# The first four heads scored in pairs, two key tiles of one pair in a step

## What is computed

```python
# x: (8, 512, 256)   ctx: (8, 1601, 256)   16 heads of 16 columns
q = split_heads(layernorm(x) @ Wq.T + bq)
k = split_heads(ctx @ Wk.T + bk)
v = split_heads(ctx @ Wv.T + bv)
attn = softmax(einsum('bhqd,bhkd->bhqk', q, k) / 4)
x = x + merge_heads(einsum('bhqk,bhkd->bhqd', attn, v)) @ Wo.T + bo
gate, y = fp4_linear(layernorm(x), w_gate), fp4_linear(layernorm(x), w_up)
x = x + fp4_linear(silu(gate) * y, w_down)   # 704 wide, blocks of 16 rounded to FP4
```

## Time and profile before

| what | value |
|---|---|
| median of 3 runs | 1728.53 us (1728.46 to 1728.66) |
| the profiled execution | 1727.77 us |
| its span, first to last instruction | 1725.6 us |
| PE busy | 1653.8 us, 96% of the span |
| DVE busy | 1428.7 us, 83% |
| ACT busy | 1132.9 us, 66% |
| mean granted TensorE clock | 0.989 |
| first score product | 69.89 us into the span |

### The profile page before, as it was taken

One profiled execution on the slowest core, in us unless ns is written; L12 is line 12 of the kernel. 1 busy time (PEld: TensorE's weight loads), 2 busy tenths in 40 slices (PEclk: granted clock), 3 DMA queues, 4 the chain that ended last, 5 costly groups with the idle time before them and its releaser, 6 DMA issues.

```text
span 1725.6 us, 27107 instructions
## 1 busy us (share of the span) xinstructions
PE 1653.8 (96%) x9484; PEld 665.2 (39%) x9484; DVE 1428.7 (83%) x2084; ACT 1132.9 (66%) x2295; POOL 548.5 (32%) x661
## 2 busy tenths in 40 slices
PE   6799899999999999999999999999999999989978
PEld 4332234334433344333443344333443344323345
DVE  5878988988798978898889887899878987898347
ACT  3377677766777667776677667776677766666731
POOL 5238520732025320543107320263304431013301
PEclk9899999999999999999999999999999999999989
DMA  6735332431335333142323323243222323200000
GB/s 164 164 76 136 70 70 44 107 93 33 56 66 120 63 63 57 49 116 46 78 45 85 102 41 58 48 118 85 57 55 55 79 48 67 45 8 10 13 22 13
DMA packets 106772, 117.53 MB, mean 68 GB/s; under 512 B 23237, under 2 KB 88141, under 8 KB 106637
## 3 DMA queue, kind: packets, MB, share of 16 engines
q1 hardware_dynamic: 101808, 111.62, 30.6%
q10 hardware_dynamic: 4828, 4.18, 1.0%
HBM read 76.78 MB, written 30.16 MB: 62 GB/s over the span
## 4 chain that ended last, share of the span: by engine, by line
PE 82%; DVE 11%; ACT 4%; issue 2%; DMA 1%; POOL 0%; ACTq 0%; SPq 0%; DVEq 0%
PE pvb L871 21%; PE st L837 20%; PE mx L856 11%; PE misc L758 7%; DVE cmx L1120 5%; PE misc L720 5%; PE misc L713 4%; PE misc L779 3%; ACT prob L1042 2%; PE misc L771 2%; PE misc L699 2%; PE misc L767 1%; PE misc L799 1%; PE misc L808 1%; DVE ht L1149 1%
## 5 line engine op out<-in xcount | busy, mean ns | idle before, releaser
L1042 ACT ACTIVATE prob<-st 128x512 f32<-128x512 f32 (+1 forms) x1591 | 867.4, 599 | 374.8 <-PE st L837 371.4
L1120 DVE TENSOR_REDUCE cmx<-mx 128x2 f32<-128x1024 f32 x768 | 905.1, 1219 | 149.5 <-PE mx L856 144.2
L837 PE MATMUL st<-qstack,kstack 112*128 112x512 bf16 (+1 forms) x1591 | 497.0, 384 | 8.9 <-ACT prob L1042 2.4
L871 PE MATMUL pvb<-prob,vv 128*32 128x512 f32 (+1 forms) x3328 | 444.2, 606 | 0.6 <-ACT prob L1042 0.6
L837 PEld LDWEIGHTS st<-qstack,kstack 112*128 112x128 bf16 (+1 forms) x1591 | 128.1, 98 | 464.8 <-issue 238.3
L856 PE MATMUL mx<-kstack,qstack 48*128 48x512 bf16 (+1 forms) x2048 | 256.5, 336 | 17.5 <-DVE cmx L1120 17.4
L1377 POOL TENSOR_TENSOR ht<-ht,rh 128x352 f32<-128x352 f32 (+1 forms) x78 | 57.0, 754 | 417.6 <-DVE rh L1096 417.6
L758 PE MATMUL misc<-wguT,rowsT 128*128 128x352 f32 x456 | 153.7, 458 | 0.0
L1369 POOL TENSOR_TENSOR ht<-ht,mt 128x352 f32<-128x352 f32 (+1 forms) x136 | 120.9, 911 | 69.4 <-DVE mt L1275 60.0
L856 PEld LDWEIGHTS mx<-kstack,qstack 48*128 48x128 bf16 x2048 | 59.5, 94 | 197.6 <-issue 137.3
L1383 POOL TENSOR_TENSOR cin<-cin 128x400 f32<-128x400 f32 (+1 forms) x60 | 55.7, 929 | 250.7 <-ACT cin L967 250.6
(11 more groups left out here) (192 smaller groups left out, 1556.1 us busy)
## 6 DMA issues: line engine op xcount, KB each, us to landing
kstack<-scr_k SPq DMA_DIRECT2D x378, 100.1 KB, 4.4
scr_k<-cin SPq DMA_DIRECT2D x48, 300.0 KB, 4.4
qstack<-scr_q SPq DMA_DIRECT2D x372, 32.0 KB, 1.9
cin<-ctx_in SPq DMA_DIRECT2D x16, 512.0 KB, 5.4
scr_q<-qp SPq DMA_DIRECT2D x16, 384.0 KB, 4.3
scr_k<-cin SPq DMA_DIRECT2D x16, 300.8 KB, 4.9
xn<-x SPq DMA_DIRECT2D x8, 512.0 KB, 4.0
cin<-ctx_in SPq DMA_DIRECT2D x16, 256.0 KB, 5.7
```

The lines of the kernel that those rows point to most:

```text
L837: mm(score_bank(it, n, h)[0:KROWS[kt], :], kstack[:, hd, KOFF[kt]:KOFF[kt] + KROWS[kt]], qstack[:, hd, :], start=True, stop=True).then_inc ...
L871: last = mm(pvb[2 * D * h:2 * D * (h + 1), :], vv[0:w, kt, (HG * g + h) // 2, D * (h % 2):D * (h % 2 + 2)], prob[0:w, n % 2, h, :], start= ...
L1042: activate(prob[0:KROWS[kt], n % 2, 2 * pair + h, :], score_bank(it, n, 2 * pair + h)[0:KROWS[kt], :], ACT.Exp, scale=SCALE).then_inc(exp_ ...
L1120: v.tensor_reduce(cmx[:, g % 2, h0:h0 + 2, at:at + 1], products, op=ALU.max, axis=AX.X).then_inc(max_free, 1)
```

## The change

The four heads of group 0 of batch 0 alone are worked on in another order. In the iteration "first", the steps 0 to 12 still do four scores each, but step n takes two tiles of keys of one pair of heads: 2n and 2n + 1 of heads 0 and 1 up to tile 12, which is the first half of step 6, and then the 13 tiles of heads 2 and 3. So the first step needs only the maxima of heads 0 and 1.

- `place` gives the group, the tile and the head of a score; `scores`, `exps` and `weighted` use it.
- The prologue makes reductions 0 to 17 (`MADE`). The first 5 steps (`FOURS`) make four each and the next 8 three each.
- A new job `nmh` at the prologue's step 41 turns, copies, splits and sends the maxima of heads 0 and 1, with a gathering reduction after reduction 12. `first_maxima_in` sends their three rows between the third and the fourth piece of `keys_out`.
- The job `nm` of group 0 moves to step 2 of "first"; `maxima_in` of heads 2 and 3 is the first thing that SP does in "first". It is needed in step 6.
- Since a step uses two tiles of values, `v` 4 to 7 are made two in a step in the prologue, and `v` 8 to 12 move from steps 0 to 4 to steps 2 to 6. `ctx2` moves from steps 0 to 3 to steps 4 to 7 and `xnT` 0 from step 6 to step 7.

```diff
-AHEAD = 4
-CATCH_UP = 2 * M_LEAD - M_GROUP - AHEAD
+AHEAD = {n: ([2 * n, 2 * n + 1] if n < M_HEADS // 2 else [M_HEADS - 1]) for n in range(M_HEADS // 2 + 1)}
+AHEAD.update({7: [13], 8: [14, 15], 9: [16, 17]})
+MADE = 18
+FOURS = 5
+CATCH_UP = 2 * M_LEAD - MADE - FOURS
...
+FIRST_SLOTS = {
+    **SLOTS, 0: ([], []), 1: ([], []), 2: ([("v", 8, "att")], [("nm", 0, "once")]), 3: ([("v", 9, "att")], []),
+    **{4 + j: ([("v", 10 + j, "att")], [("ctx2", j, "once")]) for j in range(3)},
+    7: ([("xnT", 0, "early")], [("ctx2", 3, "once")]),
+}
...
-    47: ([("nm", 0, "early")], []),
+    41: ([("v", 2, "early"), ("v", 3, "early")], [("nmh", 0, "early")]),
...
-    2: [("late", "values", 4)], 3: ...
+    2: [("late", "values", 4), ("once", "nm", 0)], 3: ...
...
-    47: [("early", "nm", 0)], 50: [("next", "apply", 1)],
+    41: [("early", "nmh", 0)], 43: [("next", "apply", 1)],
...
+def place(kind, n, h):
+
+    g, kt = divmod(n, NKT)
+    if kind == "first" and g == 0:
+        pair, kt = divmod(2 * n + h // 2, NKT)
+        return g, kt, 2 * pair + h % 2
+    return g, kt, h
...
             if it.kind == "first" and n < CATCH_UP:
-                first, number = M_GROUP + AHEAD + 3 * n, 3
+                first, number = (MADE + 4 * n, 4) if n < FOURS else (MADE + FOURS + 3 * n, 3)
...
+            def first_maxima_in():
+                sp.wait_ge(nmp_half, 1)
+                for a in range(3):
+                    sp.dma_start(qstack[MAXROW + a:MAXROW + a + 1, 0:2, :], nmp[0:2 * QT, 0, a, :]).then_inc(nm_half, 16)
...
-                keys_out(it, 1, range(4))
+                keys_out(it, 1, range(3))
+                first_maxima_in()
+                keys_out(it, 1, range(3, 4))
                 ctx_in_rows(it, "next")
-                maxima_in(it, 0, "early")
...
+                if it.kind == "first":
+                    maxima_in(it, 0, "att")
...
-                    if kt == 0 and pair == 0:
-                        pe.wait_ge(nm_row[g], it.count("att", 48, 48))
+                    g, kt, k = place(it.kind, n, 2 * pair)
+                    if kt == 0 and k in (0, 2 * pair):
+                        if it.kind == "first" and g == 0 and k == 0:
+                            pe.wait_ge(nm_half, 48)
+                        else:
+                            pe.wait_ge(nm_row[g], it.count("att", 48, 48))
...
+                    if it.kind == "pre" and j == M_HEADS - 1:
+                        dve.wait_ge(max_free, M_HEADS)
+                        v.tensor_reduce(nmx[:, 0, 0:2 * QT].rearrange("p (h t) -> p h t", h=2), cmx[:, 0, 0:2, :].rearrange("p h (t n) -> p h t n", t=QT),
+                                        op=ALU.max, axis=AX.X, negate=True).then_inc(nmx_half, 1)
...
+                def split_first_maxima():
+
+                    rows = slice(0, 2 * QT)
+                    dve.wait_ge(free["nmh"], 1)
+                    v.tensor_copy(nmp[rows, 0, 0, :], nmf[rows, :]).then_inc(nmh_step, 1)
...
```

More of the change, by code:

```diff
@@ L153, in slots @@
 def slots(kind, n):
-    return {"pre": PRE_SLOTS, "tail": TAIL_SLOTS}.get(kind, SLOTS).get(n, ([], []))
+    return {"pre": PRE_SLOTS, "first": FIRST_SLOTS, "tail": TAIL_SLOTS}.get(kind, SLOTS).get(n, ([], []))
 PER = {}
@@ L161 @@
 PER["ctxT"] = NKT
+PER["nmh"] = 1
 PAIRS = (NKT + 1) // 2
@@ L419, in maxima @@
             if it.kind == "first" and n < CATCH_UP:
-                first, number = M_GROUP + AHEAD + 3 * n, 3
[L421 to L425, removed]
+                first, number = (MADE + 4 * n, 4) if n < FOURS else (MADE + FOURS + 3 * n, 3)
+            wanted = range(first, first + number) if it.kind != "pre" else AHEAD.get(n - STEPS + M_LEAD, [])
             if part not in it.parts:
@@ L428, in maxima @@
             found = []
-            for q in range(first, first + number):
+            for q in wanted:
                 g, j = divmod(q, M_GROUP)
@@ L865, in weighted @@
                         pe.wait_ge(s_ones, 1)
-                    if n == 0 or 8 <= n < NKT:
+                    if it.kind == "first" and n <= NKT // 2:
+                        pe.wait_ge(free["v"], min(2 * n + 2, NKT))
+                    elif it.kind != "first" and (n == 0 or 8 <= n < NKT):
                         pe.wait_ge(free["v"], it.count(part, NKT, n + 1 if n else 8))
@@ L870, in weighted @@
                     for h in range(HG):
-                        last = mm(pvb[2 * D * h:2 * D * (h + 1), :], vv[0:w, kt, (HG * g + h) // 2, D * (h % 2):D * (h % 2 + 2)], prob[0:w, n % 2, h, :], start=(kt == 0), stop=(kt == NKT - 1))
+                        g, kt, k = place(it.kind, n, h)
+                        w = KROWS[kt]
+                        last = mm(pvb[2 * D * k:2 * D * (k + 1), :], vv[0:w, kt, (HG * g + k) // 2, D * (k % 2):D * (k % 2 + 2)], prob[0:w, n % 2, h, :], start=(kt == 0), stop=(kt == NKT - 1))
                     last.then_inc(pv_done, 1)
@@ L971, in take @@
                         last = copy(vpart[0:w, j, :, 0:3:2, :], src[0:w, 0:E].rearrange("p (a b d) -> p a b d", a=H // 2, b=2))
+                    elif kind == "nmh":
+                        last = copy(nmf[0:2 * QT, :], src[0:2 * QT, 0:128])
                     elif kind == "nm":
+                        if part == "once":
+                            act.wait_ge(nmp_half, 1)
                         need(act, nmp_ready, c(NG, j))
@@ L1036, in exps @@
                 def exps(n, pair):
-                    kt = n % NKT
+                    w = KROWS[place(it.kind, n, 2 * pair)[1]]
                     if pair == 0:
@@ L1195, in extra @@
                         split_maxima(part, k)
+                    elif what == "nmh":
+                        split_first_maxima()
                     elif what == "values":
```

40 lines of the change are left out of this document (27 added, 13 removed).

## The result

| | before | after |
|---|---|---|
| median of 6 runs, us | 1728.47 (1725.48 to 1728.66) | 1734.73 (1732.57 to 1736.09) |
| the profiled execution, its span, us | 1727.77, 1725.6 | 1732.57, 1730.4 |
| first score, us | 69.89 | 61.66 |
| first score of step 5, us | 93.47 | 90.11 |
| first score of step 13, us | 123.22 | 130.63 |

The ratio is 1.0044, with a 95% interval of 1.0034 to 1.0054: the change makes the kernel slower by 6.3 us. 1725.1 was forecast, with 1728.8 as the upper end of the range. The first score came nearly where I put it (60.6). By step 5 the kernel after was 5.4 us behind the forecast (84.7), and by step 13 it was 10.8 behind (119.8).

The account below looks back on a forecast made before the run. PE was taken to bound the steady steps, DVE the prologue. Scores start 9.3 us sooner, 5.9 are paid back, step 13 comes 3.4 earlier: 1728.53 - 3.4 = 1725.1 us, range 1722.0 to 1728.8.

Parts of the forecast that it names:

- The first score: End of the prologue: first score at 60.6, just behind the rows' landing at 60.4, 9.3 us earlier than before.
- low clock: From the first score, after PE's idle wait: 1.2 GHz for about 5 us, costing 0.6 us on DVE's start.
- From step 5 on PE is the bound; its steps are built from like ones: Steps 5 to 12: PE takes 34.9 us, estimated from like earlier steps, plus 0.2 allowed, so step 13 starts at 119.8.
- rival B: Steps 1 to 3: PE stays at 1.2 GHz while products wait for DVE, 7.6 us lost, 1732.7; chance 0.11.
- C: Steps 0 to 4: DVE starves, 0.6 us more a step, or rows land at 62.9; 1727.8, no change; chance 0.21.
- the order within a ring: Before the first score: engines take descriptors in order, so the rows land just behind the second write of keys, at 60.4.
- Rival A: Before the first score: writes of keys don't delay the rows, landing 56.8, first score 57.05; 1722.9; chance 0.16.
- DVE bounds steps 0 to 4: Catch-up: DVE sets the pace from 62.0 for 24.63 us, and PE may leave step 4 at 84.7.
- The rows of heads 2 and 3: Second rows of maxima: last sent at 79.1, landed by 87.4, needed near 90 in step 6; costed at nothing.
- nothing changes: After step 13: the gain of 3.4 us is neither multiplied nor lost.

Follow-up runs that it names:

- 7: Kernel after with fillers on PE: 18 identity products before the first score, 3, 3, 2, 1 before pair products 20 to 23; 1730.28 us, ratio 1.0023.
- experiment 6: Kernel after with four quarters of `pvb` in every step (result not the reference's) and all the fillers in PE's waits; 1724.68 us against 1726.00, ratio 0.9991.
- experiment 5: Kernel before with identity products filling PE's four waits at the end of the prologue; 1724.93 us against 1726.00, ratio 0.9991.
- experiment 9: Kernel after with each of the first 13 steps' value products ordered a, a, b, b instead of a, b, a, b; 1731.19 us (one run).
- experiment 3: Kernel after with the three rows of the first two heads' maxima issued from ACT's queue instead of SP's; 1737.27 us (one run).
- 8: Kernel after with the first two heads' rows issued before all four writes of keys instead of behind the third; 1733.07 us (one run).
- experiment 1: Kernel after with each step's four value products writing four quarters of `pvb` (result not the reference's); 1727.47 us against 1727.16, ratio 1.0003.
- experiment 4: Kernel after with 18 identity products filling PE's wait for the first two heads' rows; 1731.85 us against 1727.16, ratio 1.0035.

## Why the prediction was wrong, step by step

Step 13 came at 130.63 and not at 119.8. The table splits the 10.83 us, from one execution of each kernel:

| term | us | from |
|---|---|---|
| value products on two quarters, steps 5-12 | 5.14 | 40.52 - 35.38 (7 less 6) |
| the same, steps 0-4 | 1.27 | 25.39 - 24.12 (7 less 6) |
| low clock, steps 0-4, beyond the 0.6 forecast | 2.46 | 28.45 - 25.39 - 0.6 (after less 7) |
| the rows landed later | 1.06 | 61.66 - 60.6 |
| the rest of the steps | 0.90 | 24.12 + 35.38 - (59.2 - 0.6) |

**"From step 5 on PE is the bound; its steps are built from like ones": this is the step that failed.** PE was the bound, but the steps were not like. I counted tiles of values, context jobs and pair products of a step and took its value products as unchanged, since their number and shape are. Between the first score and step 13 there are 12 sets of them; 11 write two quarters and cost 1.91 in place of 1.07, 9.2 us of PE time. 6.4 of it showed. Most of the rest lay where PE waits when the products are short: from the first score to step 13 it is idle for 3.5 us in experiment 6 and for 1.3 in 7. The earlier trace rows could not show it; what could was in the change: `place` gives a step two heads, and `pvb` is addressed by the head.

The traces show this as four instructions side by side when they write four different quarters (a set of eight in 1.06 us) and two by two when they write two (1.91). The page "TensorEngine Tiling (Array Packing)" of the Trainium skill (section "Tiling Modes") lists four tiles for the 128 x 32 shape, each tied to its PSUM partitions, and "TensorE: Matmul & The Clock Gate" (Part 3, "Packing small matmuls — row/col tiling") says that matmuls on different tiles run at the same time and that the partition at which an output starts is its column tile. By these rules two quarters can feed only two tiles, and the trace agrees (1.91 by 1.06 is 1.80). That was the rule that spoke against this change, and I didn't weigh it. Whether it is the array's columns that are busy, or the adding into the same partitions of PSUM, these runs can't tell: one goes with the other here, and it wasn't tried apart.

**The low clock: mechanism right, size wrong.** I forecast 1.2 GHz from the first score for 5 us, at 0.6 us. It was there for 11 us, to 72.9, and cost 3.06. My case against the rival B was that the clock came back after 5 us of work before; here PE's work after the restart was broken by waits for DVE (the last, 0.90 us, ahead of 66.04), and the clock came back while PE ran without a gap from there. The first set of value products fell into that stretch (3.52 us), which is what made DVE idle for 2.54. The signs that I had named for the rivals B (a low clock after 70) and C (a first reduction of step 0 after 63; it began at 63.25) both came. B's mechanism did hold for steps 0 and 1, but not for 2 and 3, so its price of 7.6 us did not come. That its time, 1732.7, lies near the measured 1734.7 is luck: most of the difference is the quarters', which no rival had. C, in which the order of the jobs starves DVE, did not come: the 2.54 is DVE's one gap clearly over 0.6 us behind its first reduction, and it lies where PE ran slow. The earlier trace rows had the price in another form, which I didn't read as one: the kernel before lost 2.0 us to the same thing, as experiment 5 shows.

**The first score: right within 1.1 us, which is inside what it varies (60.48 in experiment 9).** The wait was put down to the rows of `nmp`, and 61.66 stood close to 60.6. Its parts were off both ways: SP began the rows at 54.83 and not at 53.25, 1.0 us of this because the split began only at 53.14, behind reduction 13 (forecast 52.15), and 0.6 because the second instruction of the split took 0.86 us (53.38) and not 0.28; the last row then took 4.97 us and not 5.85. The reason that I took from the page "DMA: Bandwidth & Descriptors" of the Trainium skill (section "Queues, rings and completion order"), the order within a ring, isn't borne out as the decisive one: a ring without writes of keys (3) brought the rows no earlier, and no write of keys ahead of them (8) brought the first score 3 us forward. Rival A, rows in 2.3 us behind these writes, did not come.

**Held as forecast:** DVE bounds steps 0 to 4, 24.12 us when the two causes are gone, and steps 5 to 12 take 35.38. That 24.12 meets the 24.1 of the forecast is in part luck: DVE began 0.96 us behind the first score and not 1.4, because the clock was at 1.00, and the stretch from there to step 5 took 23.16 and not 22.7. The rows of heads 2 and 3 are issued from 81.94 on, and PE doesn't wait for them in step 6.

**From step 13 to the end** I said that nothing changes. One more set of slow products, that of step 12, runs inside step 13 (133.48, 1.91 us) and makes the offset of 7.4 us 8.2. At the end of the attention it is 7.5 (1648.69 and 1656.17), but the spans differ by 4.8 only. The last stretch, of the kernel after and of the kernel before:

```profile
1664.00:1730.00 66.00, 48.34 (x208) 34.37 (x206) 51.65 (x112) 10.09 (x24) 7.78 (x8) 0.92 0.04 13
```

```profile
1656.00:1725.00 69.00, 51.63 (x210) 36.28 (x208) 51.83 (x112) 10.09 (x24) 7.78 (x8) 0.85 0.04 12
```

The same work went with a clock of 0.92 and of 0.85 in these two executions. This varies from one execution to the next (each kernel's runs spread over 3 us), so the medians, 6.3 us apart, are the better measure of what the change does.

## What to carry to other kernels

When a change alters which outputs lie next to each other on TensorE, ask of each narrow product into which 32 partitions of PSUM it writes: number and shape may be the same and the time nearly double. Where work is moved to a stage in which TensorE waits for another engine, look for the granted clock there first; fillers in its waits brought step 13 of the kernel before 2.0 us forward, and left the whole reordering, freed of its quarters, only 0.3 there and nothing at the end of the attention. And compare what a stage starts earlier with the next transfer it will need.

## What the runs showed of the hardware that I had not expected

- Four products of 128 x 32 by 512 in float32 (eight instructions) take 1.06 us over four quarters of a bank's partitions and 1.91 over two, in the order a, b, a, b as in a, a, b, b (1.92). At 1.2 GHz they take 1.94 (experiment 1) and 3.52.
- Waits of 0.46 and 0.74 us a little over 1 us apart were followed by a fall of the clock from 1.00 to 0.50 (experiment 4); waits of 0.42 and 0.74 us as far apart were not (experiment 6). With fillers in such waits it stayed at 1.00 for 14 us in which PE was busy 84% of the time (experiment 5, from 62 to 76).
- With 300 KB writes of keys in flight, the last 2 KB row took 4.37 us on a queue of its own (experiment 3) and 4.97 behind them on the same queue.
- In every run of the changed order one small instruction of DVE's split was slow while an operation of GpSimd ran beside it (53.15 to 54.10 in the kernel after): the subtraction took 0.86 us in place of 0.28, or, in experiments 1 and 3, the conversion ahead of it 0.87 and 0.77 in place of 0.20. The cause was not tested.
